# Input and weights also handed over features first: no flips of them on the chip, and a new prologue

## The chip, the cores and the metric

The kernel runs on 1 core of one Trainium2 chip. The metric is the time of one execution in microseconds (us). The kernel before took 2877.07 us in the median of 3 runs (2870.65 to 2880.16).

## The reference, cut to what matters

One transformer layer over 16 batches of 1024 tokens with 256 features, all in float32, 16 heads of 16 features, a gated feed-forward layer of 768 hidden features with integer weights.

```python
q, k, v = (split_heads(x @ W.T + b) for W, b in ((Wq, bq), (Wk, bk), (Wv, bv)))
scores = einsum('hbnd,hbmd->hbnm', k, q) / 16       # 16 heads of 16 features
out = moveaxis(einsum('hbnm,hbmd->hbnd', softmax(scores), v), 0, 2).reshape(16, 1024, 256) @ Wo.T + bo
x = layernorm(x + out)
gate, up = x @ (w_gate / 127).T, x @ (w_up / 127).T # 256 -> 768, weights are int32 in -127..127
x = layernorm(x + (silu(gate) * up) @ (w_down / 127).T)
```

## The kernel before, in words

TensorE contracts over the partition axis, so that x and every weight must lie with their features on partitions before they can be multiplied. The kernel before loads them with tokens (or output features) on partitions and flips them in 128x128 blocks on TensorE (`flip`, line 930, a transpose against the identity `ident`), into PSUM; VectorE copies them to SBUF.

**The loop.** A batch is 64 steps, one for each 128 tokens of one half of the keys for one group of four heads. In a step, `score` issues four score matmuls (two units), ScalarE takes the exponential of each unit (128x1024, line 556) into `probs`, and two steps later `products` multiplies `probs` with `v`, for two steps at a time, in every even step. So two steps are one period of TensorE: 8 score matmuls, 32 product matmul instructions, and between them what else is due. PSUM: four banks for scores, one (`ACC`) for the products, three (`RING`) for everything else, taken in turn by *items*.

**The items.** `Plan` (lines 94 to 153) spreads the other work over the odd steps of the 64. In batch b it holds the projections of batch b+1 (`xT`: flips of x, scaled by VectorE into `xT`; `qk`; `norm`: largest norms of q and k; `v`) and what follows the attention of batch b-1 (`out`, `x1T`, `gate`, `up`, `down`). Their order is written out by hand in `FULL` (lines 84 to 86); for batch 0 the plan is `PRE_PLAN`, for batch 15 `POST_PLAN`, and after batch 15 the rest runs alone (the tail). An item waits until the item three before it has been drained from its bank. VectorE, GpSimd and ScalarE each follow an order sorted by times in steps that `Plan` gives: `xT` is drained by VectorE at L676, `qk` by ScalarE (L528) and VectorE (L660), and GpSimd squares it (L445); the upper part of h is made by VectorE (L714, L718), its lower part by GpSimd (L466, `split_low`), and `down` items 0 and 2 wait for all lower parts of their half. After each `out` and `down` item comes a layer norm: VectorE statistics, GpSimd's power (L459), VectorE normalising (L738).

**Maxima.** The scale of a batch comes from the largest |x|, and a flag from the largest norms. Both need a maximum over partitions, which GpSimd makes with `partition_all_reduce` (L437, L453). Within the loop GpSimd does both when it comes to an entry of time 46 (`POOL_REDUCE`) or later, ahead of that entry; VectorE uses them at steps 50 (`DECIDE`) and 54 (`SCALE`).

**Queues.** All DMAs are issued by SyncE in one order. At the end of batch b it stores the result of batch b-1 (it waits for `y_ready`), waits for the store to land, reloads `x_res` (to which GpSimd adds the bias, L479, and which `out` items then need), and only then, for batch b+1, loads the stack of the second head group and the next `x_pre`.

**The prologue.** Before batch 0: four weights flipped, bounds of the weights over partitions by GpSimd, x flipped, its maximum over partitions, scale, `FIRST` (the projections of batch 0), `norm` drained only after the scale of batch 1 has been found, the flag, the shift rows (`prepare_shift`, L788), which SyncE loads; then the integer weights to float, their maximum over partitions, and 36 flips of them. Then TensorE reads whether the integer weights are wide and takes one of two copies of the whole program (`everything(3)` or `everything(1)`), batch 0 among it.

Of the kernel before, what the change touches and what calls it, by code (L numbers as in the profile page):

```python
# [7 lines left out]
BF16 = mybir.dt.bfloat16  # L8
# [6 lines left out]
P = 128  # L15
# [51 lines left out]
QK = 8  # L67
# [3 lines left out]
COST = {"xT": (4, 109), "x1T": (4, 109), "qk": (2, 868), "norm": (1, 330), "v": (4, 434), "out": (4, 434),  # L71
        "gate": (4, 216), "up": (4, 216), "down": (24, 108)}
PRE, POST = ("xT", "qk", "norm", "v"), ("out", "x1T", "gate", "up", "down")
# [6 lines left out]
def gate_up(*gs):  # L80
# [8 lines left out]
FIRST = (some("xT", 0, 1, 2, 3) + some("qk", *range(QK)) + some("norm", 0, 1) + some("v", 0, 1, 2, 3))  # L89
ONLY_PRE = FIRST  # L90
# [12 lines left out]


class Plan:

    def __init__(self, items, prepares):
# [5 lines left out]
        for n, (kind, _) in enumerate(items):  # L113
            count, cost = COST[kind]
            steps = [2 * min(STEPS // 2 - 1, (at + cost * i + cost // 2) * (STEPS // 2) // total) + 1
# [11 lines left out]
        for n, (kind, j) in enumerate(items):  # L127
# [29 lines left out]
FULL_PLAN, PRE_PLAN, POST_PLAN = Plan(FULL, PREPARES), Plan(ONLY_PRE, PREPARES), Plan(ONLY_POST, PREPARES[:-1])  # L157
# [7 lines left out]
def build(nc, x, Wq, bq, Wk, bk, Wv, bv, Wo, bo, w_gate, w_up, w_down, out):  # L165
    ctx = ExitStack()
    with ctx:  # L167
# [11 lines left out]
        x_pre = sb("x_pre", [P, TILES, DIM])  # L179
# [29 lines left out]
        row_sums = sb("row_sums", [P, 4])  # L209
        bounds = sb("bounds", [P, 3])  # L210
# [27 lines left out]
        w_flat = probs[:, 0:2, :, :].rearrange("p a g n -> p (a g n)")  # L238
        w4_raw = w_flat[:, 0:2048].rearrange("p (w c n) -> p w c n", w=4, c=CHUNKS)
        w_rest = w_flat[:, 2048:2048 + HALF]  # L240
        ints = ffn[:, 0:3 * 1536]
        gate_raw = ffn[:, 0:1536].rearrange("p (c n) -> p c n", c=HCHUNKS)
        up_raw = ffn[:, 1536:3072].rearrange("p (c n) -> p c n", c=HCHUNKS)
        down_raw = ffn[:, 3072:4608].rearrange("p (c n) -> p c n", c=CHUNKS)
# [23 lines left out]
        bounds_ready, bounds_reduced = sem("bounds_ready"), sem("bounds_reduced")  # L268
# [5 lines left out]
        setup_fill, setup_free = sem("setup_fill"), sem("setup_free")  # L274
# [14 lines left out]
        x_v = x.rearrange("b (p t) d -> b p t d", t=TILES)  # L289
        out_v = out.rearrange("b (p t) d -> b p t d", t=TILES)  # L290
# [5 lines left out]
        def _(sp):  # L296
            for n, w in enumerate((Wq, Wk, Wv, Wo)):
                sp.dma_start(w4_raw[:, n, :, :], w.rearrange("(c p) k -> p c k", p=P)).then_inc(weights_loaded, 16)
            sp.dma_start(x_pre[:, :, :], x_v[0]).then_inc(x_pre_loaded, 16)
            with nc.allow_non_contiguous_dma(reason="three bias vectors, once"):  # L300
                sp.dma_start(bqk[:, 0:2], bq.rearrange("(c p) -> p c", p=P)).then_inc(biases_loaded, 16)
                sp.dma_start(bv_col[:, :], bv.rearrange("(c p) -> p c", p=P)).then_inc(biases_loaded, 16)
                sp.dma_start(bqk[:, 2:4], bk.rearrange("(c p) -> p c", p=P)).then_inc(biases_loaded, 16)
# [41 lines left out]
            for idx in range(4):  # L345
                store_parts(0, idx)
            for s in range(2):
                sp.wait_ge(parts_stored[s], 32)
# [818 lines left out]
```

## Time and profile before

| | us |
|---|---|
| median of 3 runs | 2877.07 |
| the profiled execution, its own time | 2875.62 |
| its span, first to last instruction | 2873.80 |
| TensorE busy (matmul) | 2688.1 (94%) |
| ScalarE busy | 2133.8 (74%) |
| VectorE busy | 1363.5 (47%) |
| GpSimd busy | 539.2 (19%) |

The span is that of the trace; the execution's own time is 1.82 us longer. In the trace PE is TensorE's matmuls, PEld its weight loads, DVE is VectorE, ACT is ScalarE, POOL is GpSimd, SP is SyncE. L927 is the helper through which all matmuls go and L930 the one of all flips, so one has to go by the operands' names: `ident,x_pre` are the flips of x, `ident,ffn` those of the integer weights, `kstack,qstack` the scores, `probs,v` the products.

### The profile page before, as it was taken

The numbers are of one execution on the slowest core, as the hardware profiler recorded it, in microseconds if no ns is written. First come the engines' busy times: TensorE is split into PE (matmuls) and PEld (weight loads), VectorE is DVE, ScalarE is ACT, GpSimd is POOL, SyncE is SP. The second block draws the span as 40 slices with busy tenths as digits, with TensorE's granted clock in tenths as the row PEclk, the third lists the DMA queues.
The fourth block names the chain that finished last, engine by engine and source line by source line (L and its number), as shares of the span: only waits on it lengthen the run. The fifth ranks groups of instructions, "written<-read, shape, count | busy, mean of one in ns | idle before, by whom it ended". The sixth has DMA issues, their size and how long they took to land. (4 is left out here: it accounts for less than half of the span.)

```text
span 2873.8 us, 47670 instructions
## 1 busy us (share of the span) xinstructions
PE 2688.1 (94%) x17592; PEld 985.2 (34%) x17592; DVE 1363.5 (47%) x2845; ACT 2133.8 (74%) x2369; POOL 539.2 (19%) x544
## 2 busy tenths in 40 slices
PE   5689999999999999999999999999999999999996
PEld 3223233332333333243333333333233332333333
DVE  4313554455454545545444454545544454454437
ACT  0587777777777777777777777777877777777881
POOL 1001111121121212211121111212211121111113
PEclk7899999999999999999999999999999999999998
DMA  3111121021210212021021211202121021211100
GB/s 119 46 46 57 38 68 43 23 82 30 72 46 30 73 31 81 29 67 53 20 83 30 67 44 42 68 24 79 31 67 49 17 89 29 66 46 38 32 16 37
DMA packets 80081, 144.13 MB, mean 50 GB/s; under 512 B 27584, under 2 KB 30272, under 8 KB 75584
## 3 DMA queue, kind: packets, MB, share of 16 engines
q1 hardware_dynamic: 79808, 140.46, 15.7%
q8 instruction: 174, 2.85, 0.4%
q14 instruction: 99, 0.81, 0.1%
HBM read 88.48 MB, written 50.33 MB: 48 GB/s over the span
## 5 line engine op out<-in xcount | busy, mean ns | idle before, releaser
L556 ACT ACTIVATE probs<-psum 128x1024 f32<-128x1024 f32 x2048 | 1994.0, 1025 | 632.2 <-PE psum L927 631.4
L927 PE MATMUL psum<-probs,v 128*32 128x512 f32 x8192 | 992.2, 602 | 0.0
L927 PE MATMUL psum<-kstack,qstack 51*128 51x512 f16 x4096 | 678.7, 385 | 84.7 <-ACT probs L556 61.5
L927 PEld LDWEIGHTS psum<-kstack,qstack 51*128 51x128 f16 x4096 | 146.2, 93 | 825.7 <-ACT probs L556 456.4
L927 PEld LDWEIGHTS psum<-probs,v 128*32 128x32 f32 x8192 | 214.8, 109 | 516.7 <-issue 512.5
L466 POOL TENSOR_TENSOR ffn<-h,ffn 128x512 f16<-128x512 f32 x192 | 221.4, 1155 | 688.3 <-DVE ffn L718 586.9
L445 POOL TENSOR_TENSOR squares<-parts 128x512 bf16<-128x512 f16 x128 | 133.0, 1039 | 689.6 <-DVE parts L660 689.6
L669 DVE SCALAR_TENSOR_TENSOR tanh_out<-tanh_out,psum 128x512 f32<-128x512 f32 x192 | 130.6, 680 | 224.8 <-ACT tanh_out L537 224.4
L794 DVE STREAM_TRANSPOSE flipped<-psum 128x512 f32<-128x512 f32 x128 | 91.7, 716 | 296.9 <-PE psum L927 296.7
L660 DVE SCALAR_TENSOR_TENSOR parts<-psum,scales,parts 128x512 f16<-128x512 f32 x128 | 95.5, 746 | 285.7 <-ACT parts L528 285.7
L927 PE MATMUL psum<-ffn,upT 128*128 128x512 f16 x768 | 213.5, 381 | 4.1 <-DVE tanh_out L669 3.5
L927 PE MATMUL psum<-downT,ffn 128*128 128x256 bf16 x1536 | 187.4, 274 | 25.1 <-POOL ffn L466 25.1
L927 PE MATMUL psum<-ffn,gateT 128*128 128x512 f16 x768 | 204.2, 382 | 3.7 <-DVE tanh_out L669 3.3
L714 DVE SCALAR_TENSOR_TENSOR h<-tanh_out,h_scale,psum 128x512 f32<-128x512 f32 x192 | 143.4, 747 | 101.3 <-PE psum L927 91.5
L459 POOL TENSOR_TENSOR rstd<-vareps,minus_half 128x2 f32<-128x2 f32 x128 | 90.8, 710 | 445.0 <-DVE vareps L731 445.0
L927 PEld LDWEIGHTS psum<-downT,ffn 128*128 128x128 f16 x1536 | 142.0, 98 | 82.4 <-issue 66.4
L738 DVE TENSOR_SCALAR x_res<-x_res,meanvar,rstd 128x256 f32<-128x256 f32 x256 | 93.2, 407 | 126.3 <-POOL rstd L459 126.1
L537 ACT ACTIVATE tanh_out<-psum 128x512 f32<-128x512 f32 x192 | 112.5, 594 | 45.7 <-PE psum L927 44.6
L927 PE MATMUL psum<-WoT,outT 128*128 128x256 f32 x512 | 128.2, 394 | 9.2 <-DVE x_res L694 8.5
L927 PE MATMUL psum<-WvT,xT 128*128 128x256 f32 x512 | 129.8, 397 | 7.2 <-DVE norms L679 7.2
L927 PE MATMUL psum<-xT,WqT 128*128 128x512 f32 x256 | 129.5, 629 | 0.0
L927 PE MATMUL psum<-xT,WkT 128*128 128x512 f32 x256 | 128.0, 613 | 0.0
(95 smaller groups left out, 1613.6 us busy)
## 6 DMA issues: line engine op xcount, KB each, us to landing
parts_dram<-parts SPq DMA_DIRECT2D x64, 512.0 KB, 2.8
qstack<-parts_dram SPq DMA_DIRECT2D x384, 64.0 KB, 2.2
kstack<-parts_dram SPq DMA_DIRECT2D x384, 64.0 KB, 2.1
x_pre<-in_L_attn_x SPq DMA_DIRECT2D x17, 1024.0 KB, 4.9
x_res<-in_L_attn_x SPq DMA_DIRECT2D x16, 1024.0 KB, 5.3
out<-x_res SPq DMA_DIRECT2D x32, 512.0 KB, 2.7
kstack<-shift_parts SPq DMA_DIRECT2D x384, 4.0 KB, 1.7
ffn<-in_L_ffn_w_gate SPq DMA_DIRECT2D x1, 768.0 KB, 8.9
```

The costliest lines, as they stand in the source:

```text
L445: nc.gpsimd.tensor_tensor(squares[:, idx, cols], parts[:, idx % 2, 0, cols], parts[:, idx % 2, 0, cols], ALU.mult).then_inc(squares_ready, 1)
L459: nc.gpsimd.tensor_tensor(rstd[:, tiles], vareps[:, tiles], minus_half[:, tiles], ALU.pow).then_inc(rstd_ready, 1)
L466: nc.gpsimd.tensor_tensor(hT[hf][1][:, hc, :], h32[:, g % 2, :], hT[hf][0][:, hc, :], ALU.subtract).then_inc(h_lo_ready, 1)
L537: nc.scalar.activation(tanh_out[:, g % 2, :], bank[RING + n % RINGS], ACT.Tanh, scale=0.5 * W_SCALE).then_inc(tanh_ready, 1)
L556: nc.scalar.activation(probs[:, (STEPS * b + k) % SLOTS, 2 * pr:2 * pr + 2, :], scores[pr], ACT.Exp, scale=score_scale[par]).then_inc(prob ...
L660: nc.vector.scalar_tensor_tensor(out=parts[:, idx % 2, 1, cols], in0=o, scalar=scale[:, BIAS + idx:BIAS + idx + 1], in1=parts[:, idx % 2, ...
L669: nc.vector.scalar_tensor_tensor(out=gated, in0=gated, scalar=1.0, in1=o, op0=ALU.add, op1=ALU.mult).then_inc(ring_free, 1)
L714: nc.vector.scalar_tensor_tensor(out=h32[:, j % 2, :], in0=tanh_out[:, j % 2, :], scalar=h_scale[:, 0:1], in1=o, op0=ALU.mult, op1=ALU.mul ...
L738: ins = nc.vector.tensor_scalar(x_res[:, t, :], x_res[:, t, :], meanvar[:, t, 0:1], rstd[:, t:t + 1], ALU.subtract, ALU.mult)
L794: nc.vector.transpose(flipped[:, hf, :], bank[ACC]).then_inc(acc_free, 1)
L927: return nc.tensor.matmul(o, lhsT, rhs, start=start, stop=stop)
```

## The change

The caller hands over x twice, as before and with features outermost (`x_t`), and all weights features outermost. The flips of weights and of `x_pre` go. `x_pre` now has the shape [128, 2, 1024], and VectorE scales it straight into `xT` in two operations (`scale_x`), late in the batch before, after `v` has been made from the old `xT`. The plans lose `xT`; `v` 2 and 3 move ahead of `down`; `norm` moves by a pair of gate and up items; the plan of batch 0 is squeezed into 52 steps, in which VectorE also converts the integer weights. In the prologue the maxima over partitions are made by a transpose, a reduce and a matmul with ones (`spread_maxima`), the sums of |W| by a matmul with ones. TensorE's choice between the two copies now comes after batch 0, which is there once. SyncE's and ScalarE's queues share the first loads.

```diff
-FULL = (some("xT", 0, 1, 2, 3) + some("qk", 0, 1, 2, 3) + some("out", 0, 1, 2, 3) + some("qk", 4, 5)
-        + some("x1T", 0, 1) + some("qk", 6) + some("x1T", 2, 3) + some("qk", 7) + gate_up(0, 1)
-        + some("norm", 0) + gate_up(2, 3) + some("norm", 1) + gate_up(4, 5, 6, 7, 8, 9, 10, 11)
-        + some("v", 0, 1) + some("down", 0, 1, 2, 3) + some("v", 2, 3))
+FULL = (some("qk", 0, 1, 2, 3) + some("out", 0, 1, 2, 3) + some("qk", 4, 5)
+        + some("x1T", 0, 1) + some("qk", 6) + some("x1T", 2, 3) + some("qk", 7) + gate_up(0, 1, 2)
+        + some("norm", 0) + gate_up(3, 4) + some("norm", 1) + gate_up(5, 6, 7, 8, 9, 10, 11)
+        + some("v", 0, 1, 2, 3) + some("down", 0, 1, 2, 3))
...
+FIRST = some("qk", *range(QK)) + some("v", 0) + some("norm", 0, 1) + some("v", 1, 2, 3)
...
+            if (kind, j) == ("v", TILES // 2 - 1):
+                dve += [(max(at, SCALE + 1.0) + 0.3 + 0.4 * hf, "xT", hf, n) for hf in range(HALVES)]
...
+            sp.dma_start(x_pre[:, :, :], xt_v[0]).then_inc(x_pre_loaded, 16)
+            for tile, w in ((WqT, Wq_t), (WkT, Wk_t)):
+                sp.dma_start(tile[:, :, :], w.rearrange("(c p) n -> p c n", p=P)).then_inc(qk_loaded, 16)
...
+            sp.wait_ge(x_scaled, 2)
+            sp.dma_start(x_pre[:, :, :], xt_v[1]).then_inc(x_pre_loaded, 16)
+            store_parts(0, 0)
+            store_parts(0, 1)
...
             load_stack(0, 0)
+            store_parts(0, 2)
+            store_parts(0, 3)
             load_shift(0, 0)
...
+            act.dma_start(bo_all[:, :], bo.partition_broadcast(P)).then_inc(biases_loaded, 16)
...
+            dve.wait_ge(biases_loaded, 64)
+            nc.vector.tensor_reduce(maxima[:, 1:2], bqk[:, :], AX_X, ALU.max, apply_absolute_value=True)
+            dve.wait_ge(x_pre_loaded, 16)
+            nc.vector.tensor_reduce(maxima[:, 0:1], x_pre[:, :, :].rearrange("p c n -> p (c n)"), AX_X, ALU.max,
+                                    apply_absolute_value=True).then_inc(maxima_ready, 1)
...
+            def spread_maxima(n):     # VectorE
+
+                dve.wait_ge(flip_made, n + 1)
+                then(nc.vector.tensor_reduce(maxima[0:2, 0:1], bank[2][0:2, 0:P], AX_X, ALU.max))
+                nc.vector.tensor_scalar(spread[0:2, 0:2], ident[0:2, 0:2], maxima[0:2, 0:1], None, ALU.mult
+                                        ).then_inc(diag_ready, 1)
+                dve.wait_ge(spread_made, n + 1)
...
+            def spread_maxima(n, source):     # TensorE
+
+                nc.tensor.transpose(bank[2][0:2, 0:P], source, ident[:, :]).then_inc(flip_made, 1)
+                pe.wait_ge(diag_ready, n + 1)
+                mm(bank[3][:, 0:2], ones32[0:2, :], spread[0:2, 0:2], True, True).then_inc(spread_made, 1)
...
+            def scale_x(hf, scale):
+
+                cols = slice(hf * HALF, (hf + 1) * HALF)
+                nc.vector.tensor_scalar(xT[:, :, cols], x_pre[:, :, cols], scale[:, S:S + 1], None, ALU.mult
+                                        ).then_inc(x_scaled, 1)
...
+                    if first and INTS <= k < INTS + 3:      # INTS, WMAX, WIDE = 22, 28, 56
+                        to_float(k - INTS)
+                    if first and WMAX <= k < WMAX + 3:
+                        find_wmax(k - WMAX)
+                    if first and k == WIDE:
+                        convert_weights()
...
+            for n, (kind, j) in enumerate(FIRST):
+                do_item(first_plan, n, 0, COST[kind][0], 0, 0, None, 1, True)
+                if (kind, j) == ("v", 1):
+                    pe.wait_ge(norm2_ready, 1)
+                    spread_maxima(1, norm2[:, :])
+                    pe.wait_ge(flag_ready, 1)
+                    pe.reg_load(general, flag[0:1, 0:1])
+                    prepare_shift(0, 0, 0, n + 1, n + 2 - RINGS)
...
+            batch(0, 0, True, False, 1)
             pe.wait_ge(wide_ready, 1)
             pe.reg_load(wide_weights, wide[0:1, 0:1])
-
-            pe.wait_ge(setup_free, fills)
             with pe.If_eq(wide_weights, 1):
                 everything(3)
...
+    inputs["x_t"] = x.reshape(BATCHES, P, TILES, DIM).transpose(0, 3, 2, 1).reshape(BATCHES, DIM, TOKENS)
```

The weights wanted first (Wv, Wo) and the biases are issued by ScalarE. `everything` no longer holds batch 0.

## Rows read from the trace of the kernel before

**Rows 1.** The page: busy time and share of the span.

```profile
PE 2688.1 (94%) x17592; PEld 985.2 (34%) x17592; DVE 1363.5 (47%) x2845; ACT 2133.8 (74%) x2369; POOL 539.2 (19%) x544
```

**Rows 2.** Waits of PE from 252 to 2655 us: total us, times, longest us.

```profile
PE psum L927 <- ACT probs L556: 40.1, 126, 0.7
PE psum L927 <- POOL ffn L466: 25.1, 14, 2.4
```

**Rows 3.** Busy time by stretch: length, then each engine's (instructions); PEclk, DMA, GB/s.

```profile
95.80:260.00 164.20, 144.72 (x934) 41.09 (x934) 36.30 (x72) 135.69 (x148) 14.11 (x14) 0.97 0.17 53
...
2310.00:2480.00 170.00, 163.06 (x1078) 58.27 (x1078) 82.31 (x173) 130.74 (x146) 33.41 (x33) 0.99 0.16 48
```

**Rows 4.** Timeline of the prologue: start us, length us, engine, operation [idle before].

```profile
14.19 0.16 DVE L605 TENSOR_REDUCE bounds<-bqk 128x1 f32<-128x4 f32 x1 [0.66 <-DMA bo_all<-in_L_attn_bo]
...
17.87 2.47 DVE L626 TENSOR_REDUCE xmax<-x_pre 128x1 f32<-128x512 f32 x4
...
29.97 0.38 POOL L437 PARTITION_ALL_REDUCE xmax_all<-xmax_safe  x1 [6.10 <-issue]
...
31.76 2.72 DVE L676 TENSOR_SCALAR xT<-psum,scales 128x512 f32<-128x512 f32 x4
...
33.47 9.53 PE L927 MATMUL psum<-xT,WqT 128*128 128x512 f32 x16
...
52.64 0.62 PE L927 MATMUL psum<-squares,heads 128*32 128x512 bf16 x4 [1.02 <-POOL squares L445]
...
75.91 0.22 DVE L788 MEMSET shift_parts<- 32x192 uint32 x1 [1.02 <-issue]
...
76.16 3.76 SPq L332 DMA_DIRECT2D kstack<-shift_parts  x6
...
89.95 1.88 DVE L900 CAST downT<-psum 128x512 bf16<-128x512 f32 x3
...
95.90 1.04 PE L927 MATMUL psum<-kstack,qstack 51*128 51x512 f16 x4 [5.15 <-issue]
```

**Rows 5.** The page: DMA issues, median us from issue to landing.

```profile
kstack<-shift_parts SPq DMA_DIRECT2D x384, 4.0 KB, 1.7
```

**Rows 6.** Timeline of PE where one of the full batches begins.

```profile
2309.78 0.60 PE L927 MATMUL psum<-kstack,qstack 51*128 51x512 f16 x4
...
2312.70 2.15 PE L930 MATMUL psum<-ident,x_pre 128*128 128x128 f32 x16
2314.79 0.61 PE L927 MATMUL psum<-kstack,qstack 51*128 51x512 f16 x4
2315.33 1.92 PE L927 MATMUL psum<-probs,v 128*32 128x512 f32 x16
...
2335.25 1.46 PE L927 MATMUL psum<-WoT,outT 128*128 128x256 f32 x6
```

**Rows 7.** Timeline of PE, inside the `down` items of the same batch.

```profile
2460.82 0.93 PE L927 MATMUL psum<-downT,ffn 128*128 128x256 bf16 x7 [2.39 <-POOL ffn L466]
...
2462.41 3.36 PE L927 MATMUL psum<-probs,v 128*32 128x512 f32 x16
```

**Rows 8.** Timeline of POOL, the same batch.

```profile
2429.86 0.19 POOL L451 TENSOR_TENSOR norm_safe<-norm,margin 128x2 f32<-128x2 f32 x1
...
2458.41 2.26 POOL L466 TENSOR_TENSOR ffn<-h,ffn 128x512 f16<-128x512 f32 x2 [7.35 <-issue]
```

**Rows 9.** Stretches around `down` 2 of eight batches, as in rows 3: first and last at 0.79.

```profile
1420.00:1428.00 8.00, 5.79 (x38) 2.45 (x38) 2.67 (x11) 3.56 (x5) 2.96 (x3) 0.79 0.00 0
...
2459.00:2467.00 8.00, 6.18 (x38) 2.13 (x39) 4.86 (x18) 2.80 (x3) 3.07 (x4) 0.79 0.01 2
```

**Rows 10.** Timeline, end of batch 14: last `down` item, its norm, the reloaded `x_res`.

```profile
2647.95 0.61 PE L927 MATMUL psum<-downT,ffn 128*128 128x256 bf16 x4
...
2651.56 0.73 DVE L738 TENSOR_SCALAR x_res<-x_res,meanvar,rstd 128x256 f32<-128x256 f32 x2 [0.81 <-POOL rstd L459]
...
2660.57 4.54 POOL L479 TENSOR_TENSOR x_res<-x_res,bo_all 128x2048 f32<-128x2048 f32 x1 [9.05 <-DMA x_res<-in_L_attn_x]
```

More of the change, by code:

```diff
@@ L102, with __init__ @@
 ESC_LOAD = 58
+INTS, WMAX, WIDE = 22, 28, 56
+POOL_WMAX = 40
+PRE_STEPS = 52
 class Plan:
-    def __init__(self, items, prepares):
+    def __init__(self, items, prepares, over=STEPS):
         self.items = items
@@ L114, in __init__ @@
             count, cost = COST[kind]
-            steps = [2 * min(STEPS // 2 - 1, (at + cost * i + cost // 2) * (STEPS // 2) // total) + 1
+            steps = [2 * min(STEPS // 2 - 1, (at + cost * i + cost // 2) * (over // 2) // total) + 1
                      for i in range(count)]
@@ L208, in build @@
         over = sb("over", [P, 1])
-        row_sums = sb("row_sums", [P, 4])
-        bounds = sb("bounds", [P, 3])
+        ones16 = sb("ones16", [P, P], BF16)
+        ones32 = sb("ones32", [P, P])
+        absw = sb("absw", [P, CHUNKS, 3 * DIM], BF16)
+        maxima = sb("maxima", [P, 2])
+        spread = sb("spread", [P, 2])
+        act_warm = sb("act_warm", [P, 1])
         bounds_all = sb("bounds_all", [P, 3])
@@ L367, in batch @@
                 sp.wait_ge(scores_ready, UNITS * b + 2 * PER_GROUP)
+                if first:
+                    for s in range(2):
+                        sp.wait_ge(parts_stored[s], 32)
                 load_stack(b, 2)
@@ L612, in _ @@
[L612 to L619 removed]
+            dve.wait_ge(qk_loaded, 32)
@@ L620, in _ @@
+            spread_maxima(0)
+            nc.vector.tensor_scalar(xmax_all[:, :], bank[3][:, 0:1], NORM_MARGIN, None, ALU.mult)
+            then(nc.vector.tensor_scalar(bound_slope[:, 1:2], bank[3][:, 1:2], NORM_MARGIN / TOP, 1e-25, ALU.mult,
                                          ALU.add))
@@ L841, in batch @@
                         scale_segment(j)
+                    elif kind == "xT":
+                        if not last:
+                            scale_x(j, scales[:, par, :])
                     elif kind == "x1":
@@ L858, in tail @@
                         normalise(3, int(kind == "down"), b, x1_ready if kind == "out" else y_ready)
-            for part in range(4):
-                find_xmax(0, part)
-            find_scale(0, scales[:, 0, :])
+            find_scale(scales[:, 0, :])
+            for hf in range(HALVES):
+                scale_x(hf, scales[:, 0, :])
+            for c in range(CHUNKS):
+                ins = nc.vector.tensor_scalar(bv_wide[:, c * P:(c + 1) * P], ident[:, :], 0.0, bv_col[:, c:c + 1],
+                                              ALU.mult, ALU.add)
@@ new lines, in _ @@
+                if (kind, j) == ("norm", 1):
+                    spread_maxima(1)
+                    then(nc.vector.tensor_scalar(norm2_all[:, :], bank[3][:, 0:2], NORM_MARGIN, None, ALU.mult))
+                    decide(scales[:, 0, :])
+                    dve.wait_ge(flag_ready, 1)
+                    dve.reg_load(general, flag[0:1, 0:1])
+                    prepare_shift(0, n + 2, True)
+            dve.wait_ge(wo_bv_made, 1)
+            nc.vector.tensor_tensor(bo_all[:, :], bank[ACC][:, 0:DIM], bo_all[:, :], ALU.add).then_inc(bo_ready, 1)
@@ new lines, in _, with to_float, find_wmax @@
+            dve.wait_ge(xmax_reduced, 1)
+            find_scale(scales[:, 1, :])
+            for hf in range(HALVES):
+                scale_x(hf, scales[:, 1, :])
+            def to_float(i):
+                if i == 0:
+                    dve.wait_ge(ints_loaded, 48)
+                third = ints[:, 1536 * i:1536 * (i + 1)]
+                nc.vector.tensor_copy(third, third.bitcast(I32))
+            def find_wmax(i):
+                dve.drain()
+                ins = nc.vector.tensor_reduce(wmax[:, i:i + 1], ints[:, 1536 * i:1536 * (i + 1)], AX_X, ALU.max,
+                                              apply_absolute_value=True)
+                if i == 2:
+                    ins.then_inc(wmax_ready, 1)
@@ L964, in do_item @@
                 kind, j = plan.items[n]
-                o = bank[RING + n % RINGS]
+                o = bank[RING + (start + n) % RINGS]
                 count = COST[kind][0]
```

283 lines of the change are left out of this document (122 added, 161 removed).

## The prediction, made before the changed kernel was run

> **What bounds the kernel now.** I read the page's busy shares first. TensorE is busy 94% of the span, ScalarE 74%, VectorE 47%, GpSimd 19% [rows 1]. A share over the whole span mixes stages, so next the stretches. Inside a full batch TensorE is busy 163.1 of 170 us, ScalarE 130.7 [rows 3]: TensorE is the bound of batches 1 to 14, and an instruction taken out of its stream is worth its slot. In batch 0 it is not: 144.7 of 164.2 us, beside ScalarE's 135.7, with few other items [rows 3]. Then the waits of TensorE between 252 and 2655 us: 40.1 us on the exponentials in 126 short pieces, and 25.1 us in 14 pieces, one for each full batch, on GpSimd's lower part of h [rows 2]. Last the timeline ahead of batch 0: the first score matmul starts at 95.90 us [rows 4], and until then there is a serial chain with TensorE idle for most of it. So three places can pay: the prologue, the slot of the flips, and the 14 stalls.
>
> **The prologue.** Before, the chain is: weights, flips, GpSimd's bounds, maximum of x (17.87 to 20.34), GpSimd's maximum over partitions (ends 30.35, ten microseconds later), scale, xT scaled from 31.76, first projection at 33.47 [rows 4]. After, step by step:
> - VectorE still waits for all four bias loads ahead of the maximum of x. The last, bo, arrived at about 14.1 us before [rows 4]. Now ScalarE's queue issues it, beside 4 MB of x and weights in the other. I keep 14.1; ends of what I allow are 10 and 18.
> - Reduce of the four biases 0.16, reduce of x over 2048 elements in one instruction. Four of 512 took 2.47, so 2.3: 16.6.
> - Two reduces of the sums from PSUM (512 and 256 elements, 0.62 and 0.4 by the same row) and two or three small operations, 1.3 together; the transpose by TensorE lies beneath: 17.9.
> - Reduce of 2x128, product with the diagonal, a matmul of two columns, and two small operations of 0.2: estimate 1.6, from small VectorE operations at 0.2 (the memset of 0.22 is the nearest row) and hand-overs between engines. 19.5.
> - The scale: from the end of the all-reduce at 30.35 to 31.76 it took 1.4 [rows 4]. 20.9.
> - First `scale_x`, 1024 elements from SBUF. Four of 512 from PSUM took 2.72, so two of them 1.36; I take 1.2. First projection at 22.1, against 33.47: **11.4 earlier**.
> - From the first projection to the second `norm` matmul stays 19.2 (52.64 minus 33.47), since the order ScalarE, VectorE, GpSimd of each `qk` is the same; VectorE's maxima of the next x lie in its gaps. It also waits for parts stored, as before. So 41.3.
> - From there to the memset of the shift rows it took 23.3 before (75.91 minus 52.64), two reductions by GpSimd behind one another. Now: matmuls 0.6, reduces 1.1, one `v` item on TensorE ahead of the transpose (1.7), spread 1.3, flag 0.5, register load and memset 1.2 (the idle before the memset is 1.02): 6.3 less overlap, so 5.6. 46.9.
> - Six DMAs of the shift rows: 3.76 to issue [rows 4] and 1.7 to land [rows 5]. First score at 52.5, against 95.90. The stack of the first group is issued behind parts 0 and 1 alone, some six microseconds earlier in the chain, so it is not late. What came after 76 us before, the integer weights, goes into batch 0.
>
> **Prologue: −43.4**, with ends −50 (bias at 10, no gap between engines) and −33 (bias at 18 and every hand-over twice my estimate).
>
> The Trainium skill gives scale_x less than I do ("VectorE: DVE Perf Modes", Mode 2×_2P): a float32 tensor_scalar with both operands in SBUF runs at twice the rate. By it the term would be about 0.7 instead of 1.2 and the total half a microsecond lower. No row of before shows a tensor_scalar of this size from SBUF.
>
> **Batch 0.** TensorE idles ahead of it in both versions, so it begins at the low clock in both. Its pairs of steps are bound by the coupling with ScalarE, so taking 16 flips out and squeezing the rest into 52 steps is worth nothing; bounds −4 and +5. The conversion of the integer weights on VectorE (three casts, three reduces, three casts, about 11 us) hides in VectorE's idle time: it is busy 36.3 of 164.2 us [rows 3]. If the last part, at step 56, holds up the drain of the products' bank, it costs at most 3 us.
>
> **The choice between the two copies** moves from the prologue to the end of batch 0. Before, between the end of the last cast, 91.83, and the first score matmul, 95.90, nothing else is left to do: 4.1 us [rows 4]. TensorE now pays it with the pipeline full, and what follows a stall of 2.4 us can run at the low clock: products that take 1.92 took 3.36 [rows 6, 7]. **+5.8** (4.1 and 1.7), bounds 0 and +10. In the prologue the 4.1 are gone with the rest and are in the 43.4. The Trainium skill speaks against the change here too ("Runtime: NRT & Kernel Launch", Instruction fetch mechanics): a taken branch to a target that is not at hand has to fetch its instructions by DMA before the engine goes on. The row agrees with a stall, though it doesn't say of what the 4.1 us consist.
>
> **Flips of x in the full batches.** Sixteen take a slot of 2.09 us (2312.70 to 2314.79) [rows 6]. TensorE waits neither before nor behind, so 14 batches give **−29.3**. VectorE loses four drains (2.72) and gains two scalings. These sit at step 55, far ahead of the projection at step 1 that needs them, and behind the scale, which still comes from GpSimd's all-reduces in time. Nothing of TensorE's is behind them.
>
> **The stall at `down` 2.** GpSimd enters its two all-reduces at 2429.86 with the last two lower parts of h behind them, made at 2458.41 to 2460.67 [rows 8]. `down` 2 waits 2.39 us for them [rows 7]. The change leaves GpSimd's order as it is, but two `v` items now come ahead of `down`: by the plan `down` 2 starts at step 59 instead of 55 to 57. Two more pairs of 5.3 us are more than the longest wait of 2.4, so it goes: **−25.1** [rows 2]. In five of eight batches that I looked at the clock granted around it was 0.76 to 0.79, half speed for part of the stretch [rows 9]; 0.21 of 8 us is 1.7 each. With the five that I saw: **−8.6**. What is late next: `down` 3, which now ends with the batch. Two things hang on it.
> - VectorE finishes its norm 3.7 us after the matmul (2652.29 minus 2648.56 [rows 10]), then empties the products' bank, 0.7. TensorE wants that bank 5.5 us after the batch starts (2315.33 minus 2309.78) [rows 6]. Margin about 1 us.
> - From the matmul to biased `x_res` it is 16.5 us (2665.11 minus 2648.56) [rows 10]. In a full batch the first `out` was done 26.9 us after the start (2336.71 minus 2309.78) [rows 6]; its new plan has it a pair of steps earlier, but behind the same projections, so about 25. Margin 8.5 us. In batch 15 `out` comes at once: there the biased `x_res` comes 6.5 us later than before, since `down` 3 ended 6.5 us before the batch did (2655.1 minus 2648.6, one pair and a part). The flips of x1 at steps 11 to 13 are the first that need the norms; by counting the steps up to them all but 1.3 of the 6.5 is slack: **+1.3**, bounds 0 and +6.5.
>
> **The sum**, against the profiled execution's own 2875.6: −43.4 +5.8 −29.3 −25.1 −8.6 +1.3 = −99.3, so 2776.3. The median lies 1.5 above this execution: **2778**. The tail after batch 15 keeps its order and its time.
>
> **Rivals.**
> - *A: as worked out.* 2778, own range 2762 to 2796.
> - *B: the stall at `down` 2 only moves.* TensorE waits for h or for the bank at another place, since less of its own work lies between. For it: the 40.1 us on exponentials and the margin of 1 us at the start of a batch. Against: ten microseconds of slack at `down` 2. Then the 33.7 stay: 2812.
> - *C: the prologue gives less.* The bias load late, hand-overs slow, the conversion or the branch in the way: +10 at the bounds of each: up to 2796, in A's range for the most part.
> - *D: the gain is larger.* As TensorE has fewer items, waits for exponentials shrink, or the clock doesn't fall behind the branch: 2757. For it: the bounds. Against: less work of TensorE's between two exponentials makes it wait for ScalarE rather more.
> - *E: slower than before.* `down` 3 at the end of the batch holds SyncE's queue: the store waits for its norm, behind it stand the reload of `x_res`, the stack of the second group and the next x. Each batch pays by how much the biased `x_res` comes after 25 us. To lose the 99 us, 14 batches must pay 7.1 each, so 16.5 must become 32. Just past it: 2880. Against: only a doubled chain does it, and the queue is idle otherwise.
>
> **How the numbers follow.** A (with C) 0.68, B 0.17, D 0.11, E 0.04. The range takes A, B and the near part of D: 2756 to 2813. Less than 0.3% (9 us) can't be told from no change. Only E is not faster, and a part of it would end within 0.3%: faster 0.96, same 0.01, slower 0.03.
>
> **What would show it.** First score matmul near 52 us; no matmuls of ident with x_pre; no wait of TensorE for GpSimd's lower part of h from batch 1 on; the start of one full batch to the next 4 to 5 us shorter than before (2.09, 1.8 and 0.6 from the sum, over 14 batches); an idle time of TensorE of about 4 us where batch 1 starts; a wait for the biased `x_res` in batch 15 only. Wrong would be: a first score later than 62 us; new waits of TensorE of more than 1 us per batch on the drain of the products' bank or on `x_res`; full batches less than 2 us shorter each.

## The result and the profile after

The changed kernel took 2782.49 us in the median of 4 runs (2781.8 to 2783.46), the kernel before, run beside it, 2874.41 (2870.65 to 2880.16): ratio 0.968, 95% interval 0.966 to 0.970. The forecast was 2778 with a range of 2756 to 2813. The profiled execution took 2781.8 with a span of 2779.7, against 2875.62 and 2873.8 before: 93.8 us less by their own times, 94.1 by the spans. The steps below are read from these two executions.

The page of the changed kernel, the line of engines that answers to [rows 1]:

```profile
PE 2633.4 (95%) x17294; PEld 943.7 (34%) x17294; DVE 1291.1 (46%) x2812; ACT 2132.9 (77%) x2370; POOL 543.2 (20%) x542
```

TensorE's busy time fell by 54.7 us, the span by 94.1, so 39 us went out of its idle time. Next the waits of PE in the full batches of the changed kernel (203 to 2557 us), which answer to [rows 2]:

```profile
PE psum L978 <- ACT probs L567: 52.3, 156, 1.2
PE psum L978 <- DVE tanh_out L692: 8.2, 14, 0.6
```

The wait for GpSimd's part of h is gone. The one for exponentials grew from 40.1 to 52.3 us, from 126 pieces to 156. Stretches of the changed kernel (prologue, batch 0, the 14 full batches, batch 15, tail), columns as in [rows 3]:

```profile
0.00:53.50 53.50, 29.52 (x86) 16.25 (x86) 23.26 (x52) 6.99 (x10) 15.73 (x25) 0.97 0.48 161
53.50:202.80 149.30, 127.69 (x825) 34.04 (x824) 44.12 (x88) 124.80 (x136) 13.48 (x14) 0.98 0.17 51
202.80:2557.30 2354.50, 2282.72 (x15120) 817.60 (x15120) 1110.66 (x2414) 1864.91 (x2073) 464.81 (x461) 1.00 0.17 51
2557.30:2704.30 147.00, 141.66 (x996) 47.00 (x996) 61.81 (x139) 127.11 (x138) 24.03 (x21) 1.00 0.11 32
2704.30:2779.60 75.30, 51.78 (x272) 28.85 (x270) 51.29 (x120) 9.12 (x14) 25.18 (x22) 0.83 0.09 35
```

and the same stages of the kernel before:

```profile
0.00:95.90 95.90, 44.32 (x145) 29.85 (x146) 44.95 (x81) 6.78 (x9) 13.81 (x28) 0.74 0.31 98
95.90:245.70 149.80, 131.06 (x842) 36.30 (x842) 29.96 (x62) 124.73 (x136) 13.96 (x13) 0.96 0.15 46
245.70:2655.10 2409.40, 2320.07 (x15346) 843.19 (x15348) 1177.33 (x2450) 1866.07 (x2073) 462.93 (x461) 1.00 0.16 50
2655.10:2800.50 145.40, 141.64 (x997) 46.96 (x996) 60.21 (x132) 127.10 (x138) 23.32 (x20) 1.00 0.11 29
2800.50:2873.80 73.30, 51.00 (x272) 28.86 (x268) 51.08 (x120) 9.10 (x14) 25.16 (x22) 0.84 0.10 37
```

The edges are the first score matmuls of the batches in PE's timeline, so the stages add up:

| stage | before | after | change | forecast |
|---|---|---|---|---|
| prologue | 95.9 | 53.5 | −42.4 | −43.4 |
| batch 0 and the branch behind it | 149.8 | 149.3 | −0.5 | +5.8 |
| batches 1 to 14 | 2409.4 | 2354.5 | −54.9 | −63.0 |
| batch 15 | 145.4 | 147.0 | +1.6 | +1.3 |
| tail | 73.3 | 75.3 | +2.0 | 0 |

Every full batch from 2 to 14 of the changed kernel takes 168.1 us; before, they took 170.6 to 173.7. In the 14 full batches TensorE's busy time fell by 37.4 us (2320.07 to 2282.72) and its idle time by 17.6 (89.3 to 71.8). Where it idles shows in the groups of its instructions in these two stretches (busy, mean ns | idle before). Kernel before:

```profile
L927 PE MATMUL psum<-kstack,qstack 51*128 51x512 f16 x3586 | 588.9, 384 | 57.3 <-ACT probs L556 40.5
...
L927 PE MATMUL psum<-downT,ffn 128*128 128x256 bf16 x1344 | 164.7, 274 | 25.1 <-POOL ffn L466 25.1
```

Changed kernel:

```profile
L978 PE MATMUL psum<-kstack,qstack 51*128 51x512 f16 x3584 | 584.3, 383 | 63.5 <-ACT probs L567 52.3
...
L978 PE MATMUL psum<-ffn,gateT 128*128 128x512 f16 x672 | 182.5, 380 | 8.2 <-DVE tanh_out L692 8.2
```

All idle time ahead of scores rose by 6.2 us only (57.3 to 63.5), though the part that is named for exponentials rose by 12: some short gaps got a name. Ahead of gate and up it rose by 2.4 (6.9 to 9.3).

The prologue of the changed kernel in order of time, which answers to [rows 4]:

```profile
14.95 0.69 DVE L620 SCALAR_TENSOR_TENSOR absw<-WvT 128x512 bf16<-128x512 f32 x1 [4.12 <-DMA WoT<-in_L_attn_Wo]
...
15.73 2.27 DVE L625 TENSOR_REDUCE maxima<-x_pre 128x1 f32<-128x2048 f32 x1
...
18.06 0.38 PE L994 MATMUL psum<-ident,maxima 128*2 128x128 f32 x1 [0.83 <-DVE maxima L625]
...
22.00 1.41 DVE L743 TENSOR_SCALAR xT<-x_pre,scales 128x1024 f32<-128x1024 f32 x2
22.89 5.86 PE L978 MATMUL psum<-xT,WqT 128*128 128x512 f32 x8 [2.57 <-DVE xT L743]
...
41.83 0.40 PE L978 MATMUL psum<-squares,heads 128*32 128x512 bf16 x4 [0.72 <-POOL squares L457]
...
47.68 0.22 DVE L812 MEMSET shift_parts<- 32x192 uint32 x1 [1.68 <-issue]
...
53.59 0.61 PE L978 MATMUL psum<-kstack,qstack 51*128 51x512 f16 x4
```

Each mark lies within 1.4 us of the one forecast (16.6, 22.1, 41.3, 46.9, 52.5). The DMA that VectorE waits for is not bo but Wo, one issue earlier in the same queue. TensorE's clock differs from what the prediction assumed: over the first 4 us of batch 0 it was granted 0.50 before and 1.00 in the changed kernel, and the first four scores took 1.04 us before [rows 4] and 0.61 here.

The signs that the prediction named came for the most part: no flips of x, no wait for GpSimd's part of h, no new wait for the products' bank or for `x_res` in full batches, a wait behind the biased `x_res` in batch 15 only. Full batches are 3.9 us shorter in the mean, just short of the 4 to 5 named, and where batch 1 starts TensorE idles for 1.2 us in this profile, not 4.

### The profile page after: what moved, and what is told of

Same layout as the page of the kernel before. It is cut to its first block and busy times, and to the rows that moved or that the text cites. A ratio compares the mean times of both kernels' runs of the same rounds, so it can differ in the third digit from the quotient of the medians.

```text
span 2779.7 us, 47000 instructions
## 1 busy us (share of the span) xinstructions
PE 2633.4 (95%) x17294; PEld 943.7 (34%) x17294; DVE 1291.1 (46%) x2812; ACT 2132.9 (77%) x2370; POOL 543.2 (20%) x542
## 5 line engine op out<-in xcount | busy, mean ns | idle before, releaser
L763 DVE TENSOR_SCALAR x_res<-x_res,meanvar,rstd 128x256 f32<-128x256 f32 x256 | 103.5, 447 | 73.3 <-POOL rstd L471 73.3
```

Of the source, the lines that this page charges most:

```text
L763: ins = nc.vector.tensor_scalar(x_res[:, t, :], x_res[:, t, :], meanvar[:, t, 0:1], rstd[:, t:t + 1], ALU.subtract, ALU.mult)
```

## The experiments

All ran later than the first comparison, beside the kernel before: the last three (after_again, early_norm_late, pool_margin) on one chip, the others on another. There the kernel before took 2862 to 2863 us on either chip, not 2874; on which chip the first comparison ran is not on record. "A batch" below is the mean of full batches, from first score to first score.

**The changed kernel again (after_again).** No edit.

> The changed kernel itself, unedited, beside the kernel before on this chip, where the kernel before took 2862 in the last jobs and not 2874. Theory (12 us of the first chip's difference are the low clock behind the stall at down 2, which differs from chip to chip): the changed kernel again at 2782, full batches of 168.14, and the difference to before 80, not 92. Rival (the chip is faster as a whole): the changed kernel at 2770.

2783.12 us (2781.87 to 2785.01, 5 runs) beside 2863.11: ratio 0.972 (0.971 to 0.974), 80 us. The changed kernel is the same everywhere; the kernel before differs by some 12 us between the first comparison and these. Its profile without the branch, below, suggests of what. The kernel's own later executions point the same way: their mean granted clocks are 0.984 to 0.990, that of its first profile is 0.982.

**16 flips put back at one place (flips_step1)** and **spread over the projections (flips_spread).**

```diff
                 elif kind == "qk":
...
+                    if plan is FULL_PLAN and lo == 0 and j == 0:
+                        for i in range(16):
+                            flip(o[:, i % 4 * P:(i % 4 + 1) * P], ident[:, :])
```

In flips_spread the condition on j goes and the range is 2. The projection overwrites what the flips write.

> The changed kernel (2782) with 16 flips of the identity put back ahead of the first projection of each full batch, 14 batches. Their results are overwritten. Theory A (TensorE's slot is the price, 2.09 us a batch): +29.3, a batch of 170.2 instead of 168.14, time 2812. Theory B (the 8 us that came short of the sum were flips that had hidden waits for exponentials): less than +22, since the waits for exponentials shrink again by the 0.8 us a batch by which they grew.

2807.12 us (2804.78 to 2811.22), 24 above the changed kernel. Full batches take 169.84 instead of 168.14: 1.70 each, 23.8 over 14. PE's waits are 51.6 us for exponentials, as in the changed kernel, so theory B is out: the flips hide no wait. In ten full batches PE's busy time rose by 17.0, as much as the time. But 1.70 is less than the slot of 2.09 [rows 6]. PE's timeline of this run:

```profile
2247.30 0.61 PE L978 MATMUL psum<-kstack,qstack 51*128 51x512 f16 x4
2247.84 1.97 PE L981 MATMUL psum<-ident 128*128 128x128 f32 x16
2249.64 1.88 PE L978 MATMUL psum<-xT,WqT 128*128 128x512 f32 x4
2251.45 0.61 PE L978 MATMUL psum<-kstack,qstack 51*128 51x512 f16 x4
```

Start to start the flips take 1.80 where a projection follows them in the same step, and 2.09 where they filled a step alone, with scores behind. So the stand-ins undercount what a step of flips costs by some 0.3 us. How much went from the kernel before is seen without them, further down.

> The same 16 flips a batch, but two ahead of each of the eight projections, where TensorE waits 0.22 us for an exponential in most pairs of steps. Theory A: +29.3 here too, 2812. Theory B: the flips take the place of those waits, so +5 to +20; a difference between this run and the one with all 16 at step 1 says that it matters where an instruction lies between two exponentials.

2803.48 us (2802.47 to 2805.15): 169.67 a batch, 1.53 each, 21 in all. The intervals of the two runs' ratios (0.978 to 0.981 and 0.979 to 0.982) overlap, but the batch by the trace is 0.17 shorter, the same in every batch. So where they lie matters little; waits for exponentials are 53.0 us here too.

**The order of v undone (order_back).**

```diff
-        + some("v", 0, 1, 2, 3) + some("down", 0, 1, 2, 3))
+        + some("v", 0, 1) + some("down", 0, 1, 2, 3) + some("v", 2, 3))
```

> The changed kernel with v 2 and 3 behind down again, nothing else; x is then scaled after v 3, at the end of the batch. Theory A (the order alone removed the stall at down 2): the wait for GpSimd's lower part of h is back, 1.8 us in each of 14 batches, and the low clock behind some of them: +25 to +34, 2807 to 2816. Rival: the stall went since the batches are shorter or norm comes later, not by the order of v: +0 to +5. If the late scaling of x delays the first projection as well, more than +34.

2799.73 us (2797.69 to 2805.56), 17 above the changed kernel. Waits of PE in this run, 203 to 2640 us:

```profile
PE psum L978 <- ACT probs L567: 51.4, 156, 0.6
PE psum L978 <- POOL ffn L478: 18.3, 14, 1.9
PE psum L978 <- DVE tanh_out L692: 8.2, 14, 0.6
```

The stall is back in all 14 batches, 18.3 us, about the whole of the 17 that the run costs, and the other waits are as in the changed kernel. The scaling of x comes late here too (in batch 14 at 2408.27, 0.8 us behind the first score and 2.2 ahead of the first projection), and no wait for it appears. The 18.3 are below the forecast of 25 to 34: each stall is 1.3 us in the mean instead of 1.8, and no stretch of 8 us in its full batches has a granted clock below 0.95. Batch 15 goes back to 145.4 us: its 1.6 us also come from the order.

**The order alone, in the kernel before (before_v_first).** The same edit, made to the old `FULL`.

> The kernel before with v 2 and 3 ahead of down and nothing else, flips and old prologue as they were. Theory A: no wait for the lower part of h, no low clock in the middle, -25 to -34 less what waits for exponentials take back (up to 12): 2845 to 2858 against 2874. Rival: without the earlier x the order gives nothing: within 5 us of before.

2851.82 us (2849.12 to 2854.24): ratio 0.9965 (0.995 to 0.998), 11 us, between the two theories. The wait of PE that is new in it:

```profile
PE psum L930 <- DVE xT L676: 8.6, 13, 0.7
```

No wait for h is left, but half of what it had cost on this chip, 17 us, comes back as a wait for a bank at the batch's start. VectorE's timeline there shows why: the flipped x can't be drained, since the norm of `down` 3 stands before it.

```profile
2288.45 0.74 DVE L738 TENSOR_SCALAR x_res<-x_res,meanvar,rstd 128x256 f32<-128x256 f32 x2 [0.81 <-POOL rstd L459]
2289.10 0.71 DVE L794 STREAM_TRANSPOSE flipped<-psum 128x512 f32<-128x512 f32 x1
2289.73 2.68 DVE L676 TENSOR_SCALAR xT<-psum,scales 128x512 f32<-128x512 f32 x4
```

The changed kernel has nothing to drain there: the flips are gone, and x is scaled 23.5 us ahead of the batch (2533.87 against the first score of batch 15 at 2557.39). So the order is worth its full price only together with the new handling of x. Whether the missing flips or the earlier scaling does it was not separated; order_back, where x is scaled late and nothing waits for it, speaks for the flips.

This kernel differs from the changed one in its full batches by the flips, the early x and the place of `norm`. Ten full batches of it, then of the changed kernel, columns as in [rows 3]:

```profile
300.00:2003.20 1703.20, 1650.80 (x10960) 602.43 (x10960) 808.87 (x1751) 1332.60 (x1480) 334.58 (x330) 1.00 0.17 51
```

```profile
300.00:1981.40 1681.40, 1630.41 (x10802) 583.86 (x10800) 794.72 (x1730) 1331.58 (x1481) 335.00 (x330) 1.00 0.17 52
```

TensorE's busy time is 2.04 a batch shorter, with 16 instructions fewer and the clock at 1.00 in both. That is near the slot of 2.09, and not the 1.70 of the stand-ins.

**The branch taken away (before_no_branch, after_no_branch).**

```diff
-            with pe.If_eq(wide_weights, 1):
-                everything(3)
-            with pe.Else():
-                everything(1)
+            everything(1)
```

> The kernel before without the choice between the two copies on TensorE: only the copy for weights that are not wide, straight on. Theory A (the 4.1 us between the last cast and the first score were the branch): first score matmul at 91.9 to 92.5 instead of 95.9. Rival (they are something that the branch does not cause, a wait or the fetch of the code behind it all the same): still 95 to 96.

In its timeline the cast of downT ends at 92.78 and the first score starts at 92.88, a gap of 0.1 us instead of 4.1. The whole chain ahead of it ran 1 us later than in the other profile, so the first score itself came 3.0 us earlier. 2857.76 us, one run, beside 2861.89 (2858.71 to 2869.53). The gap of 4.1 us was the branch.

```profile
90.91 1.87 DVE L900 CAST downT<-psum 128x512 bf16<-128x512 f32 x3
92.88 0.61 PE L927 MATMUL psum<-kstack,qstack 51*128 51x512 f16 x4 [1.78 <-issue]
```

Waits of PE in the same run's full batches, to be compared with [rows 2]:

```profile
PE psum L927 <- ACT probs L556: 40.7, 127, 0.7
PE psum L927 <- POOL ffn L466: 17.2, 14, 1.9
```

The stall at `down` 2 is 17.2 us here, against 25.1 in the first profile; order_back, on the same chip and with the branch, has 18.3, so the missing branch is hardly the reason. The clock differs too. I cut 250 to 2650 us into 300 stretches of 8 us and summed 8 times (1 minus granted clock): 8.5 us in the kernel before, six stretches below 0.95 at five places, which take in both of [rows 9]; 1.7 here, one stretch:

```profile
2098.00:2106.00 8.00, 6.12 (x46) 2.44 (x42) 3.17 (x12) 3.98 (x5) 2.96 (x3) 0.83 0.01 2
```

and none in the changed kernel, in either of its profiles. Together 7.9 + 6.8 = 14.7 us, which is the difference of the two spans (2873.8 and 2856.0) but for the branch, 4.1: 13.7.

> The changed kernel without the choice on TensorE. The prediction gave the branch +5.8 there; its trace shows a wait of 1.2 us at the start of batch 1. Prediction's theory: -5.8. Theory from the trace: TensorE was already waiting for ScalarE and the branch is hidden for the most part: 0 to -1.5.

2781.7 us (2778.69 to 2782.55) against the changed kernel's 2782.5 and 2783.1, measured in other comparisons: 0.8 to 1.4 us in the medians, with ranges that overlap. The branch's one record in the kernel before, then in the changed one:

```profile
L1140 PEldq COMPARE_BRANCH  x1: 3792/3792/3792, 91.9 to 91.9; - x1
```

```profile
L1189 PEldq COMPARE_BRANCH  x1: 3288/3288/3288, 199.5 to 199.5; - x1
```

What it costs there differs between profiles of the same program. PE's timeline in the first profile of the changed kernel:

```profile
200.95 0.80 PE L978 MATMUL psum<-kstack,qstack 51*128 51x512 f16 x4
202.97 0.39 PE L978 MATMUL psum<-kstack,qstack 51*128 51x512 f16 x2 [1.22 <-ACT probs L567]
```

and in after_again:

```profile
199.01 0.60 PE L978 MATMUL psum<-kstack,qstack 51*128 51x512 f16 x4
202.65 0.61 PE L978 MATMUL psum<-kstack,qstack 51*128 51x512 f16 x4 [3.03 <-issue]
203.19 3.18 PE L978 MATMUL psum<-probs,v 128*32 128x512 f32 x16
```

In the first the sequencer branches from 199.5 to 202.8, the array works until 201.75 on what had been issued, and then waits 1.22 us for an exponential; without the branch it waits 0.99 there. In the second the array idles for 3.03 us and the products behind take 3.18 instead of 1.92. I counted from the first score of batch 0 to the first projection of batch 1 (in flips_step1, to the flips ahead of it): 152.8 us without the branch, 152.7 in the first profile and 152.8 in flips_spread, 154.3 in after_again, 152.7 to 155.8 in the others with the same batch 0. So the branch costs 0 to 3.0 us by this count.

A part of that is clock. Summed as above, over stretches of 4 us, batch 0 loses 3.4 us to it without the branch and in the first profile, 1.7 in order_back, 5.1 in early_norm_late, at places that change from profile to profile. Even without the branch the last products ahead of batch 1 take 3.55 us instead of 1.92. With that taken off, 149.4 us are left without the branch, 149.3 in both profiles where the array worked on, and 150.1 to 150.9 in those where it idled for about 3 us (151.9 in pool_margin, with 3.99 of idle). So, by this estimate, 3 us of idle time cost 0.7 to 1.6, not nothing and not 3: meanwhile the waits for exponentials in batch 0 fell from 21.6 to between 20.1 and 20.4. Order_back looks free (152.7 us with 3.10 of idle) only since it lost less to the clock.

**The first maximum by GpSimd (pool_max), then with the margin multiplied there (pool_margin).**

```diff
-            spread_maxima(0)
-            nc.vector.tensor_scalar(xmax_all[:, :], bank[3][:, 0:1], NORM_MARGIN, None, ALU.mult)
+            dve.wait_ge(maxima_reduced, 1)
+            nc.vector.tensor_scalar(xmax_all[:, :], maxima_all[:, 0:1], NORM_MARGIN, None, ALU.mult)
...
+            pool.wait_ge(maxima_ready, 1)
+            nc.gpsimd.partition_all_reduce(maxima_all[:, :], maxima[:, :], P, RMAX).then_inc(maxima_reduced, 1)
```

> The changed kernel with the first maximum over partitions (x and biases) made by GpSimd's all-reduce as before, instead of transpose, reduce and matmul. Theory A: from the end of the maximum of x to the first small operation on the result it takes 2.4 us in the changed kernel, of which 1.3 lies under reduces of the sums, and took 6 to 9.5 in the kernel before: +4 to +8, first score at 57.5 to 61.5. Rival (GpSimd's all-reduce overlaps with the reduces, and it is free here): +0 to +2.

2783.06 us (2781.4 to 2784.4), the same as the changed kernel; first projection at 21.72, 1.2 us *earlier*, of which 0.3 is left at the first score (53.28). My theory falls: the matrix product is not what made this maximum fast. GpSimd's timeline of it:

```profile
18.19 0.38 POOL L447 PARTITION_ALL_REDUCE maxima_all<-maxima  x1 [9.95 <-DVE maxima L630]
```

> The changed kernel with the first maximum by GpSimd's all-reduce as in pool_max (first score 53.1), but with the multiplication by the margin on GpSimd ahead of it, as the kernel before had it. Theory (GpSimd's all-reduce is not slow, changing between an ordinary operation and an all-reduce is: 6.1 us idle before it in the kernel before): about 6 us between the multiplication and the all-reduce, first score at 58 to 60. Rival (the multiplication costs its 0.2 us): 53.3.

In pool_margin GpSimd multiplies by the margin first, with an ordinary operation, and a `pool.drain()` stands between it and the all-reduce, both as in the kernel before. 2787.96 us (2 runs), first score at 58.4. GpSimd's timeline of pool_margin:

```profile
17.91 0.20 POOL L447 TENSOR_TENSOR maxima_safe<-maxima,margin 128x2 f32<-128x2 f32 x1 [9.67 <-DVE maxima L632]
...
24.00 0.37 POOL L449 PARTITION_ALL_REDUCE maxima_all<-maxima_safe  x1 [5.90 <-issue]
```

In pool_max VectorE's reduce ends at 18.05 and the all-reduce starts at 18.19, 0.15 us later, GpSimd having been idle since 8.2. In pool_margin it starts 5.9 us after the ordinary operation's end. So what costs is not the all-reduce but having an ordinary operation right ahead of it; in pool_max the last one, a memset, lay 10 us back, and nothing was paid. Product and drain came together, and a run with one of them was not made. That it is the change of kind and not the drain is supported by the way back, which has no drain and also idles: 7.35 us from an all-reduce to the next ordinary operation [rows 8]. The kernel before paid in the chain of its prologue: 6.10 idle ahead of the all-reduce at 29.97 [rows 4], and 7.58 ahead of its margin's product at 23.70, 3.4 of them after the maximum of x was there.

**An earlier maximum (early_max).** The integer weights are loaded behind the first shift rows, Wq and Wk ahead of x, and VectorE waits only for what it reads.

```diff
+            for tile, w in ((WqT, Wq_t), (WkT, Wk_t)):
+                sp.dma_start(tile[:, :, :], w.rearrange("(c p) n -> p c n", p=P)).then_inc(qk_loaded, 16)
             sp.dma_start(x_pre[:, :, :], xt_v[0]).then_inc(x_pre_loaded, 16)
-            for tile, w in ((WqT, Wq_t), (WkT, Wk_t)):
...
-            dve.wait_ge(weights_loaded, 32)
+            dve.wait_ge(v_loaded, 16)
...
-            dve.wait_ge(biases_loaded, 64)
+            dve.wait_ge(bqk_loaded, 32)
...
             load_shift(0, 0)
+            for i, w in enumerate((gate_t, up_t, down_t)):
```

> A version meant to be better than both: the integer weights are loaded only behind the first shift rows (they are wanted at step 22 of batch 0), Wq and Wk ahead of x, Wv ahead of the biases, each with a semaphore of its own, so that VectorE waits for neither Wo nor bo. Theory A (bandwidth and the wait for Wo held the start: it ended at 14.95 us): the maximum of x ends at 10 to 12 instead of 18.0, first score at 46 to 48 instead of 53.5, time 2775 to 2778. Rival (the maximum comes earlier but the parts' stores or the stack load become the bound): -2 or less.

2775.77 us (2775.18 to 2778.3), about 7 below the changed kernel. The maximum of x ends at 11.64 instead of 18.0 and the first score comes at 47.1, both as expected. VectorE's timeline:

```profile
9.37 2.27 DVE L626 TENSOR_REDUCE maxima<-x_pre 128x1 f32<-128x2048 f32 x1
```

**norm one pair of gate and up later (early_norm_late)**, on top of early_max.

```diff
-gate_up(0, 1, 2) + some("norm", 0) + gate_up(3, 4) + some("norm", 1) + gate_up(5, 6, 7, 8, 9, 10, 11)
+gate_up(0, 1, 2, 3) + some("norm", 0) + gate_up(4, 5) + some("norm", 1) + gate_up(6, 7, 8, 9, 10, 11)
```

> The version with the early maximum (2775.8, full batches of 168.14) with norm 0 and 1 one pair of gate and up items later still. In the changed kernel TensorE waits 0.58 us for tanh and 0.62 for an exponential in the pair of steps of norm 1, the longest of the batch with 6.58. Theory A (norm between a gate and its up costs there, wherever it stands): the waits move with it, 168.1 a batch, 2776. Theory B (the place can be better): 167.5 or less a batch, -9 or more.

2762.34 us (2759.27 to 2763.39, 5 runs): ratio to before 0.964 (0.963 to 0.966), 21 us below the changed kernel beside it and below both kernels. Full batches take 166.98 instead of 168.13, 16 us over 14. Against early_max, on the other chip, the times differ by 13.4 only: batch 0 took 1.7 us more in this profile, prologue, batch 15 and tail together 1.4. Waits of PE from 197 to 2540 us:

```profile
PE psum L980 <- ACT probs L568: 33.5, 126, 0.6
PE psum L980 <- issue: 3.0, 1, 3.0
```

against, in early_max from 197 to 2550:

```profile
PE psum L980 <- ACT probs L568: 50.8, 154, 0.6
PE psum L980 <- DVE tanh_out L693: 8.2, 14, 0.6
```

The wait for tanh is gone and 17 us of that for exponentials with it. So a good part of what TensorE waits for in the changed kernel's full batches hangs on the place of `norm`, and moving it one pair of items on removes it. `norm` where it stood before the change, behind gate and up 1 and 3, wasn't tried.

## Why the prediction was right

**The prologue** (−43.4 forecast, −42.4 measured) came out by its steps. Two premises were wrong without harm. Batch 0 does not begin at the low clock in the changed kernel (granted 1.00, not 0.50). And for scale_x I took 1.2 us; two halves take 1.41 together [the row at 22.00], about 0.7 each. That is what the Trainium skill's rate (VectorE: DVE Perf Modes, Mode 2×_2P) had given; the measurement decides for it. The matrix product, which the change puts forward for the maxima, is not the reason for the first of its two gains: pool_max is as fast without it. It is that GpSimd no longer has an ordinary operation and an all-reduce right behind one another in the chain (with the drain as the rival that is left). For the maximum of the norms, which comes right behind GpSimd's squares, nothing was tried.

**Batch 0** kept its time, as forecast, within the spread that the branch and the clock make.

**The branch** is the term that failed in size: +5.8 forecast, 0 to 3.0 shown, 0.8 to 1.4 in the medians. Its length was read right: before_no_branch lacks the gap of 4.1 us, the records say 3.8 and 3.3, and after_again shows the predicted idle time and the slow products behind it. The step that failed is "TensorE now pays it with the pipeline full": I took TensorE's idle time for the kernel's. In batch 0, which I had said is set by the coupling with ScalarE, a part of it takes the place of waits for exponentials that would have come anyway (1.2 to 1.5 of about 3 us), and in two profiles TensorE had enough issued ahead to lose nothing. The Trainium skill's sentence on fetches behind a taken branch (Runtime: NRT & Kernel Launch, Instruction fetch mechanics) fits both records of 3 to 4 us; they don't say of what these consist, nor who pays.

**The flips** (−29.3) came out: 2.04 a batch less busy time between before_v_first and the changed kernel, 28.6 over 14.

**The stall at `down` 2** (−25.1) went by the order, as argued: order_back brings it back. **The low clock** behind it (−8.6) went too: 8.5 us by the 300 stretches. That size is in part luck: the prediction had looked at eight of 14 places and found five, and the six others have none. Both sizes belong to the first comparison; in before_no_branch they are 17.2 and 1.7, 14.7 less together, and the change was worth 12 us less by the medians there. Why the same program stalls less there stays open.

**What was not in the sum** is +7.6 us of idle time: 6.2 ahead of scores, 2.4 ahead of gate and up, less 1.0 that the edges leave. Rival D named the direction as the argument against itself (less work of TensorE's between two exponentials) and no place. Putting the flips back did not shrink these waits (51.6 and 53.0 us), so it is not the missing flips. before_v_first has 40.3 in 126 pieces and differs else in the early x and the place of `norm`. early_norm_late goes to 33.5 us, again in 126 pieces, and gains 16 us by `norm`'s place alone. So the change of that place, which I had left out of the prediction, is the likely cause and what I should have priced; that it makes the whole of the 7.6 is not shown.

The 14 full batches then add up in the profiles of the first comparison: busy time −8.5 by the clock and −28.9 that is left of the 37.4 read, idle time −25.1 and +7.6 (the 17.6): −54.9, against −63.0 forecast.

**Batch 15**: +1.3 forecast, +1.6 measured, and order_back gives it back. The late `x_res` is there as reasoned: biased 16.3 us after the batch's start instead of 10.0. PE's timeline of the changed kernel shows where it is paid:

```profile
2581.77 1.92 PE L978 MATMUL psum<-probs,v 128*32 128x512 f32 x16 [0.77 <-ACT probs L567]
...
2590.39 1.06 PE L981 MATMUL psum<-ident,x_res 128*128 128x128 f32 x8 [1.08 <-DVE x_res L763]
```

The flips of x1 wait 1.08 us instead of 0.27, the place that the prediction named. The other half it did not name: the products' bank is emptied 2.6 us later, since VectorE does the late `out` work first (its transpose starts at 2580.91, 23.5 us into the batch, against 20.9 before), and the products start 0.77 us late. The profile names the exponentials for that wait, but in after_again the same wait, 0.98 us, is named for VectorE's transpose.

**The tail** took 2.0 us more, forecast 0. In order_back it took 75.0 too, so it isn't the order. By the timelines 0.4 us come ahead of the flips of x1, 0.4 behind the last matmul, and 1.1 in the gate and up items: the granted clock over the first 6 us of these was 0.62, against 0.83 before. In after_again the tail is 1.1 us shorter than in the first profile, so a good half of the 2.0 is no more than what one program varies by. Why the clock rises later stays open.

**The net.** Errors of both signs: batch 0 with the branch came out 6.3 us shorter than forecast, the full batches 8.1 longer, the tail 2.0, the prologue 1.0 and batch 15 0.3 longer. That the two large ones nearly cancel is luck. It leaves 5.1 of the 5.5 between 2776.3 and the 2781.8 of the profiled execution.

## What to carry to other kernels

A stall of an engine costs less than its length where another engine sets the pace (here about 3 us of idle cost 0.7 to 1.6): read the stage's bound before the stall is added to the sum. To price a small item by putting it back, give it the slot that it had, since beside another item it costs less (1.70 against 2.04). And when an order written out by hand is touched, price every place that moved: here `norm`, moved by one more pair, was worth 16 us in the full batches, more than half of the flips.

## What the hardware did that was not expected

- An all-reduce on GpSimd took 0.4 us and came 0.15 us behind its input after idle time, and 5.9 us later behind an ordinary operation and a drain (pool_max, pool_margin).
- The branch of TensorE's sequencer took 3.3 to 3.8 us. In one profile of the changed kernel the array worked through most of it on what had been issued, in another of the same program it idled for 3.03 us. Which of the two it is goes with where the clock is low: in the first the products ahead of the branch took 3.37 us, in the other 1.92.
- Batch 0 lost 1.7, 3.4 or 5.0 us to a low granted clock, at places that differ between profiles, also of one program (order_back; the first profile and after_again; flips_step1).
- The kernel before took 2874 us in one comparison and 2862 to 2863 in three others, on two chips; its stalls (25.1 and, without the branch, 17.2 us) and the clock behind them (8.5 and 1.7 us) differ by as much as the spans of the two profiles do. The changed kernel, which has neither, took 2782.5 and 2783.1.
